# Attention output products as split f32, half a pair of heads later

## The chip, the cores and the metric

The kernel runs on one core of a Trainium2 chip. The metric is the device time in microseconds (us). Its engines are TensorE (PE in the profile, its weight loads PEld), VectorE (DVE), ScalarE (ACT), GpSimd (POOL) and SyncE (SP, which issues most transfers). Each works through its own queue in order, and they meet at semaphores.

## What is computed

Four layers follow one another over x of 4 x 1024 x 256 in f32: a gated scan, a layer of eight experts with two chosen per token, a causal attention with 16 heads of width 64, and a layer of 32 experts with four chosen. The change is in the attention:

```python
q = einsum('qdh,bcd->bhcq', Q, x) * sq
k = einsum('qdh,bcd->bhcq', K, x) * sq
v = einsum('vdh,bcd->bhcv', V, x) * sv
att = where(causal, einsum('bhcq,bhCq->bhcC', q, k) / d_query, -inf)
y = einsum('bhcC,bhCv->bhcv', softmax(att), v)
z = einsum('dvh,bhcv->bcd', W, y) * (sqrt(d_embed / d_value) / num_heads)
x = x + z
```

The last einsum is what is called the output products below: for every pair of heads (two heads of 64 values fill 128 rows) the normalised values y (128 x 1024, the tile `c_yT`) times the pair's part of W (128 x 256, the tile `c_wo`).

## The kernel before

The attention runs over 4 batches of 1024 tokens, each with 8 pairs of 2 heads. Its order is written out by hand for each engine, one function per head: `head_products` for TensorE, `head_steps` for VectorE, `head_exps` for ScalarE, `head_adds` for GpSimd, `head_operands` for SyncE. In the text an even head is the first of its pair (h = 0), an odd head the second (h = 1).

While head H has its probabilities made, its successors are already begun. On TensorE, one head is, in order: transposed score blocks 3, 4, 5 of H (`scores_t`, L2517 and L2518) between score chunks M4, M5, M6 of head H+1 (`scores`, L2494), projection steps 0, 1, 2 of head H+2 (`project`, L2481) around M7, the second half of the output products if the head is odd, M8, the denominators (L2546), four outputs y of H (`outputs`, L2537), blocks 6 to 8 with M9 to M11, four more outputs, a transpose of the row maxima (L2501), blocks 9 to 11, projection steps 3 to 5, the first four score chunks N0 to N3 of head H+2, blocks 0 to 2 of H+1, the last four outputs, and, if the head is even, the first half of the output products of the pair before (`z_of`, L2564).

A score chunk exists only so that VectorE can take its row maximum (`maximum`, L1873 for a plain chunk, L1880 for a masked one). Chunks, output products, denominators and some transposes take turns in a ring of three PSUM banks. The tables of `batch_order` and `turn_tables` deal out banks in the order in which the names stand, so M7 uses the bank of M4 again, whatever else comes before M4. TensorE may write a bank only after its last reader has added one to that bank's semaphore:

```python
pe.wait_ge(s_turn[use[0]], use[1])
pe.matmul(PS[:, TURN_BANK[use[0]], 0:max(w, 256)], ...).then_inc(s_cS, 1)
```

On VectorE the end of an even head is: maxima of N0 and N1, `normalise_y` of the pair before (L1893: c_yT times the inverses of the denominators, 128 x 1024), maxima of N2 and N3, two low parts of the next queries and keys (`split_lo`, L1851), and `add_z` of output products 0 and 1 (L1916: a bank added to two tiles of x). The next thing is the maximum of M4 for the following head. In the first batch a low part of projection weights (`low_qk`, L1856) stands between, and its high part (`high_qk`, L1190) closes the head on ScalarE.

On ScalarE the end of a head is the high parts of the next queries and keys (L1274) and the probabilities 0 to 2 of the next head (L1283); the next head begins with probability 3 and with taking y of the head before (L1265).

Output products are plain f32: one of them, 128 x 128 by 128 x 256, shows as two weight loads and two matmuls of 256 columns. There are 8 per pair, in 4 units of two. Products of split operands (high part rounded to f32r, low part the rest, three terms) are used for the projections and in the first expert stage (L2400 and L2403), where the high part is a ScalarE copy (L1140) and the low part a VectorE subtraction (L1742).

The last pair of a batch has its output products after the batch's heads, all four units in a row.

## Time and profile before

| | |
|---|---|
| time, median of 3 runs | 2092.15 us (2087.59 to 2097.59) |
| time of the profiled execution | 2105.81 us, its span 2104.1 us |
| busy share of the span: PE, PEld, DVE, ACT, POOL | 88%, 68%, 70%, 54%, 56% |
| attention, from about 665 to 1860 us | 1195 us |
| mean granted clock of TensorE | 0.937 |

The span is the time from the first to the last instruction of the profiled execution. Busy times of TensorE are of pipelined instructions, so the starts and ends of neighbours tell more than the duration of one.

### The profile page before, as it was taken

The page shows a single profiled execution, that of the slowest core. Times are in us where ns is not written, and L with a number is a line of the kernel's source. Part 1 is how long each engine was busy: PE and PEld are TensorE (multiplying, and loading weights), DVE is VectorE, ACT ScalarE, POOL GpSimd, SP SyncE. Part 2 cuts the span into 40 slices and gives each one's busy share as a digit, 9 for nine tenths or more (in the row PEclk, how much of TensorE's full clock was granted, in tenths as well). Part 3 has the DMA queues.
Part 4 walks back from the last instruction along what each step waited for, and adds up shares of the span by engine and source line. Part 5 has one row for each costly group of instructions (what it writes and reads, how often), then busy time and mean ns, then how long its engine had stood idle before and what let it go on. Part 6 is the DMA issues. An engine that isn't in the chain of part 4 may idle for free. (4 is left out here: it accounts for less than half of the span.)

```text
span 2104.1 us, 40780 instructions
## 1 busy us (share of the span) xinstructions
PE 1843.9 (88%) x12355; PEld 1438.9 (68%) x12356; DVE 1478.3 (70%) x3795; ACT 1141.9 (54%) x2322; POOL 1182.8 (56%) x1159
## 2 busy tenths in 40 slices
PE   5852999999779999999999999999999999973870
PEld 2542888888657677777777787777787777743650
DVE  6865777777567887756878756887757787653663
ACT  5322555555456566656665646656646656522760
POOL 4355232333306566636687836687836687825782
PEclk9865999999989999999999999999999999986995
DMA  9762533333331121202121102121211121122979
GB/s 338 244 206 88 129 51 54 51 53 53 61 110 52 56 59 52 61 26 60 46 82 52 50 28 60 52 58 44 53 30 54 52 59 52 30 95 84 200 127 262
DMA packets 215684, 177.34 MB, mean 84 GB/s; under 512 B 85442, under 2 KB 200727, under 8 KB 214880
## 3 DMA queue, kind: packets, MB, share of 16 engines
q1 hardware_dynamic: 177904, 138.78, 22.1%
q0 software_dynamic: 28656, 27.61, 8.5%
q10 hardware_dynamic: 8960, 8.92, 1.2%
q8 instruction: 84, 1.38, 0.3%
q14 instruction: 80, 0.66, 0.1%
HBM read 95.05 MB, written 80.72 MB: 84 GB/s over the span
## 5 line engine op out<-in xcount | busy, mean ns | idle before, releaser
L957 POOL TENSOR_TENSOR c_den_late<-c_den_late,c_p 128x512 f32<-128x512 f32 (+3 forms) x384 | 410.3, 1068 | 129.5 <-ACT c_p L1283 83.9
L1283 ACT ACTIVATE c_p<-PS 128x512 f32<-128x512 f32 (+3 forms) x768 | 343.2, 491 | 206.6 <-PE PS L2518 99.8
L2537 PE MATMUL PS<-c_p,c_vh 128*64 128x256 f32 (+3 forms) x3072 | 292.5, 333 | 0.5 <-ACT c_yT L1265 0.5
L2517 PE MATMUL PS<-c_q,c_k 128*128 128x512 f32 (+2 forms) x768 | 283.3, 373 | 2.8 <-ACT c_p L1283 1.7
L2494 PE MATMUL PS<-c_k,c_q 128*128 128x512 f32 (+2 forms) x768 | 268.6, 364 | 8.4 <-DVE c_max L1873 3.3
L2518 PE MATMUL PS<-c_q,c_k 128*128 128x512 f32 (+2 forms) x768 | 258.3, 348 | 0.0
L893 POOL DMA_INDIRECT acc<-b_y,b_tok x71 | 111.9, 1576 | 259.6 <-ACT b_y L1149 235.1
L2537 PEld LDWEIGHTS PS<-c_p,c_vh 128*64 128x64 f32 x3072 | 194.3, 137 | 87.6 <-issue 20.8
L1274 ACT ACTIVATE c_q<-PS 64x512 fp32r<-64x512 f32 x256 | 151.3, 591 | 158.2 <-PE PS L2481 147.0
L1873 DVE TENSOR_REDUCE c_max<-PS 128x1 f32<-128x512 f32 x256 | 175.3, 685 | 46.6 <-PE PS L2494 44.3
L957 POOL TENSOR_TENSOR c_den<-c_den,c_p 128x384 f32<-128x384 f32 (+2 forms) x192 | 141.4, 737 | 108.6 <-ACT c_p L1283 83.4
L1880 DVE CUSTOM_DVE_ANT_0 PS<-PS,c_maskq,c_max 128x128 f32<-128x128 f32 (+3 forms) x256 | 142.7, 558 | 82.5 <-PE PS L2494 47.9
L1880 DVE CUSTOM_DVE_ANT_0 PS<-PS,c_maskq 128x128 f32<-128x128 f32 (+3 forms) x256 | 122.5, 509 | 109.3 <-PE PS L2494 102.4
L2494 PEld LDWEIGHTS PS<-c_k,c_q 128*128 128x128 f32 x768 | 145.9, 190 | 46.9 <-DVE c_max L1873 8.8
L926 POOL DMA_INDIRECT routed<-r_rows,r_slot x128 | 128.6, 1004 | 61.7 <-DVEq L1992 34.4
L2517 PEld LDWEIGHTS PS<-c_q,c_k 128*128 128x128 f32 x768 | 144.7, 188 | 23.4 <-ACT c_p L1283 3.5
L2518 PEld LDWEIGHTS PS<-c_q,c_k 128*128 128x128 f32 x768 | 145.0, 189 | 8.9
L1742 DVE TENSOR_TENSOR b_w_lo<-b_w3T,b_w_hi 128x1024 fp32r<-128x1024 f32 x71 | 87.0, 1225 | 89.9 <-ACT b_w_hi L1140 89.9
L952 POOL TENSOR_TENSOR c_den_late<-c_p 128x512 f32<-128x512 f32 x64 | 81.4, 1272 | 100.1 <-PE PS L2546 82.8
L2381 PE MATMUL PS<-b_w12h,b_tT_hi 128*128 x284 | 124.0, 437 | 5.4 <-DVE b_tT_lo L1735 2.6
L2564 PE MATMUL PS<-c_wo,c_yT 128*128 128x256 f32 x512 | 124.6, 388 | 1.3 <-DVE c_yT L1893 1.3
L996 POOL DMA_INDIRECT acc<-d_y,d_tok x64 | 100.6, 1572 | 40.0 <-ACT d_y L1462 20.4
(313 smaller groups left out, 4345.7 us busy)
## 6 DMA issues: line engine op xcount, KB each, us to landing
c_vh<-c_v SPq DMA_DIRECT2D x64, 256.0 KB
c_rrow<-rden SPq DMA_DIRECT2D x63, 256.0 KB, 3.4
routed<-b_empty SPq DMA_DIRECT2D x32, 289.0 KB, 9.4
d_xe<-routed SPq DMA_DIRECT2D x32, 289.0 KB
b_xt<-routed SPq DMA_DIRECT2D x71, 130.0 KB, 2.1
b_w12T<-in_w12T_dram SPq DMA_DIRECT2D x16, 512.0 KB, 13.9
d_acc<-acc SPq DMA_DIRECT2D x16, 512.0 KB, 8.9
c_st_hi<-wqk_split SPq DMA_DIRECT2D x48, 128.0 KB
```

The source lines that it names most:

```text
L926: pool.indirect_dma_start(routed1, bass.IndirectOffsetOnAxis(ap=r_slot[n][:, j // K1, j % K1:j % K1 + 1], axis=0), r_rows[n][:, j // K1, : ...
L957: pool.tensor_tensor(den[:, off:], den[:, off:], p, ALU.add).then_inc(s_cPa, 1)
L1274: act.activation(dst, src, ACT.Copy).then_inc(s_cqs, 1)
L1283: act.activation(c_p[:, P_AT[h][m]:P_AT[h][m] + WIDTH[m]], PS[:, ST_BANK[m % STB], skip:skip + WIDTH[m]], ACT.Exp, scale=ATT_SCALE).then_i ...
L1873: dve.tensor_reduce(dst, src, AX_X, ALU.max).then_inc(s_turn[bank], 1)
L1880: dve.tensor_tensor_reduce(src, src, c_maskq[:, 512 - w:512], 1.0, dst if c else BIG, ALU.add, ALU.max, dst).then_inc(s_turn[bank], 1)
L2381: pe.matmul(PS[:, 2 * j + c, :], b_tT[0][:, j, k, :], b_w12h[k][:, cols], start=(k == 0), stop=False)
L2494: pe.matmul(PS[:, TURN_BANK[use[0]], 0:max(w, 256)], c_q1[h][:, t * P:(t + 1) * P], c_k1[h][:, c * 512:c * 512 + max(w, 256)], start=True, ...
L2517: pe.matmul(PS[:, bank, 0:n], c_k1[h][:, j * P:(j + 1) * P], c_q1[h][:, q], start=True, stop=False)
L2518: ins = pe.matmul(PS[:, bank, 0:n], c_k2[h][:, j * P:(j + 1) * P], c_q2[h][:, q], start=False, stop=not diagonal)
L2537: ins = pe.matmul(dst, c_vh[h][:, j, :], columns[:, :, a, :], start=(j == 0), stop=(t0 == 3))
L2564: ins = pe.matmul(PS[:, TURN_BANK[use[0]], a * D:(a + 1) * D], c_yT[q][:, t * P:(t + 1) * P], c_wo[q][:, :], start=True, stop=True)
```

## The change

The output products of all pairs but a batch's last are made of parts. ScalarE gets `split_y` at the end of each even head but a batch's first: it waits until the pair before is normalised, and copies c_yT and c_wo to their high parts `c_yTh` and `c_woh`. VectorE gets `low_y` in the place where `add_z` of units 0 and 1 stood: it waits for both copies and subtracts, to `c_yTl` and `c_wol`. TensorE runs `z_of_parts`, three products of 256 columns for each one of before, and later: units 0 and 1 stand in the odd head where units 2 and 3 stood, units 2 and 3 at the end of the odd head. `add_z` moves along, and the ring's tables with it. A batch's last pair stays as it was.

Beside this, tiles get other places in SBUF (`xn1` now shares memory with rows that are scattered, and `make_xn` waits for those scatters; `r_swb` shares memory with later tiles), and two semaphores of the first expert stage become one that ScalarE and VectorE raise in turn.

```diff
--- before.py
+++ after.py
@@ -242,7 +242,9 @@
         TURNS = len(TURN_BANK)
         Y_BANK = 6
         at[0] = arena_at
+        c_wol = [nc.alloc_sbuf_tensor_at(f"c_wo_lo_{n}", [P, D], F32R, offset=at[0] + n * 4 * D) for n in range(2)]
         c_wo = [place(f"c_wo_{n}", [P, D]) for n in range(2)]
+        c_woh = place("c_wo_hi", [P, D], F32R)
         c_xT = [place(f"c_xT{n}", [P, KD, S], F32R) for n in ("_hi", "_lo")]
         c_st = [[place(f"c_st{n}_{h}", [P, KD, P], F32R) for n in ("_hi", "_lo")] for h in range(2)]
         c_stf = [nc.alloc_sbuf_tensor_at(f"c_stf{h}", [P, KD, P], F32, offset=at[0] - 4 * KD * P * (3 - 2 * h)) for h in range(2)]
...
@@ -532,6 +536,10 @@
 
         ROUTE_AT = (0, 5)
 
+        def z_split(b, hp):
+
+            return b * (NPAIR - 1) + hp
+
         def batch_order(route, nxt):
 
 
@@ -540,9 +548,9 @@
                 follows, more, zs = nxt or hd < NH - 1, nxt or hd < NH - 2, hd >= 2
                 fetch = nxt and hd == NH - 2
                 order = ["M4", "M5", "M6"] * follows + ["X0", "X1", "D"] * fetch + ["M7"] * follows
-                order += ["Z2", "Z3"] * (zs and hd % 2 == 1) + ["M8"] * follows + ["D"] * (hd > 0 and not fetch)
+                order += ["Z0", "Z1"] * (zs and hd % 2 == 1) + ["M8"] * follows + ["D"] * (hd > 0 and not fetch)
                 order += ["M9", "M10", "M11"] * follows + ["X2", "X3"] * fetch + ["T"] * follows
-                order += ["N0", "N1", "N2", "N3"] * more + ["Z0", "Z1"] * (zs and hd % 2 == 0)
+                order += ["N0", "N1", "N2", "N3"] * more + ["Z2", "Z3"] * (zs and hd % 2 == 1)
                 if route:
                     for a in ROUTE_AT:
                         order += ["U0", "U1"] * (hd == a) + ["U2"] * (hd == a + 1) + ["U3"] * (hd == a + 3)
...
@@ -1202,6 +1210,10 @@
 
                     act.wait_ge(s_dxs, batch * 32 - 32)
                     act.sem_inc(s_pass, 1)
+                if g == 1 and not (isinstance(batch, int) and batch <= 1):
+
+                    act.wait_ge(s_scat[0], (batch - 1) * (16 * G * K1) + SCAT0)
+                    act.sem_inc(s_pass, 1)
                 for q in range(G):
                     t = batch * QT + (g * G + q)
                     act.activation(xn[g][:, q, :], tile_of(t, 0), ACT.Identity, bias=shifts[:, bass.ds(t, 1)],
@@ -1264,6 +1276,16 @@
                     dst = yT[h * DQ:(h + 1) * DQ, c * 512:(c + 1) * 512].rearrange("p (t a q) -> p t a q", a=2, q=DQ)[:, :, a, :]
                     act.activation(dst, PS[a * DQ:(a + 1) * DQ, Y_BANK, c * 256:(c + 1) * 256].rearrange("p (t q) -> p t q", q=DQ),
                                    ACT.Copy).then_inc(s_cyn, 1)
+
+            def split_y(b, hp):
+
+                pair, k, n = b * NPAIR + hp, z_split(b, hp), hp % 2
+                act.wait_ge(s_cz, pair * (QT // 2) + QT)
+                act.wait_ge(s_cym, pair + 1)
+                act.sem_inc(s_pass, 1)
+                act.activation(c_yTh[:, :], c_yT[n][:, :], ACT.Copy).then_inc(s_cyp, 1)
+                act.wait_ge(s_cwo, pair * 16 + 16)
+                act.activation(c_woh[:, :], c_wo[n][:, :], ACT.Copy).then_inc(s_cyp, 1)
 
             def split_hi(H, h, c, part):
 
@@ -1341,6 +1363,8 @@
                 if follows:
                     for m in (0, 1, 2):
                         probabilities(H + 1, 1 - h, m)
+                if h == 0 and hp:
+                    split_y(b, hp - 1)
                 if splits(b, hd + 3):
                     high_qk(H + 3, pair + (1 + h), 1 - h)
                 if nxt and NH - 4 <= hd < NH - 2:
...
@@ -1906,6 +1930,13 @@
                     cols = slice(c * 512, (c + 1) * 512)
                     dve.wait_ge(s_cD, H + (3 + c + 1))
                     dve.tensor_tensor(yT[DQ:P, cols], yT[DQ:P, cols], PS[DQ:P, 4 + c, :], ALU.mult).then_inc(s_cym, 1)
+
+            def low_y(b, hp):
+
+                k, n = z_split(b, hp), hp % 2
+                dve.wait_ge(s_cyp, 4 * k + 2)
+                dve.tensor_tensor(c_yTl[n][:, :], c_yT[n][:, :], c_yTh[:, :].bitcast(F32), ALU.subtract).then_inc(s_cyp, 1)
+                dve.tensor_tensor(c_wol[n][:, :], c_wo[n][:, :], c_woh[:, :].bitcast(F32), ALU.subtract).then_inc(s_cyp, 1)
 
             def add_z(b, pair, units, table):
 
@@ -2040,7 +2071,7 @@
                     invert(H - 1, 1 - h, table)
                 maxima(7)
                 if h == 1 and zs:
-                    add_z(b, pair - 1, (2, 3), table)
+                    add_z(b, pair - 1, (0, 1), table)
                 maxima(8)
                 if hd and not fetch:
                     invert(H - 1, 1 - h, table)
@@ -2068,7 +2099,9 @@
                 for k in range(2 * more):
                     split_lo(H + 2, h, 1, k)
                 if h == 0 and zs:
-                    add_z(b, pair - 1, (0, 1), table)
+                    low_y(b, hp - 1)
+                if h == 1 and zs:
+                    add_z(b, pair - 1, (2, 3), table)
                 if splits(b, hd + 3):
                     low_qk(H + 3, 1 - h)
                 routing(4)
...
@@ -2565,6 +2598,19 @@
                                     c_wo[q][:, :], start=True, stop=True)
                 ins.then_inc(s_cz, 1)
 
+            def z_of_parts(b, hp, n, use):
+
+                k, q = z_split(b, hp), hp % 2
+                pe.wait_ge(s_turn[use[0]], use[1])
+                pe.wait_ge(s_cyp, 4 * k + 4)
+                for a in range(2):
+                    rows = slice((2 * n + a) * P, (2 * n + a + 1) * P)
+                    z = PS[:, TURN_BANK[use[0]], a * D:(a + 1) * D]
+                    pe.matmul(z, c_yTh[:, rows], c_woh[:, :], start=True, stop=False)
+                    pe.matmul(z, c_yTh[:, rows], c_wol[q][:, :], start=False, stop=False)
+                    ins = pe.matmul(z, c_yTl[q][:, rows], c_woh[:, :], start=False, stop=True)
+                ins.then_inc(s_cz, 1)
+
             def transpose_rows3(g, n, table):
 
                 pe.wait_ge(s_dxn, g * G + G)
@@ -2615,7 +2661,7 @@
 
                 def z_units(*units):
                     for n in units * zs:
-                        z_of(pair - 1, 1 - hp % 2, n, table[f"Z{n}"])
+                        z_of_parts(b, hp - 1, n, table[f"Z{n}"])
 
                 def outputs_of(r):
                     for m in range(r * ROUND, (r + 1) * ROUND):
@@ -2642,7 +2688,7 @@
                     maxima(7)
                     projections(1)
                     if h == 1:
-                        z_units(2, 3)
+                        z_units(0, 1)
                     projections(2)
                     maxima(8)
                     if hd:
@@ -2683,10 +2729,8 @@
                         scores_t(H + 1, 1 - h, m)
                     mask_t(0, 1, 2)
                 outputs_of(2)
-                if h == 0 and zs:
-
-                    pe.wait_ge(s_cym, pair)
-                    z_units(0, 1)
+                if h == 1:
+                    z_units(2, 3)
                 if route:
                     for n, a in enumerate(ROUTE_AT):
                         g = b * 2 + (n - 2)
```

## Rows read from the trace of the kernel before

**Rows 1.** Windows of the attention: busy us of each engine (x instructions), granted clock.

```profile
core 0: us, PE busy (x) PEld busy (x) DVE busy (x) ACT busy (x) POOL busy (x), PEclk, DMA share, GB/s
...
665.00:930.00 265.00, 256.96 (x1872) 194.21 (x1872) 202.72 (x449) 160.71 (x353) 164.12 (x170) 1.00 0.19 53
...
1242.00:1555.00 313.00, 310.04 (x2259) 240.70 (x2258) 230.28 (x552) 191.40 (x411) 215.56 (x224) 1.00 0.18 49
```

**Rows 2.** TensorE's own waits over the four batches (two of the list).

```profile
engine line waited for: us in total, times, longest us
PE PS L2501 <- DVE c_max L1880: 8.0, 6, 1.8
...
PE PS L2494 <- DVE c_max L1873: 1.7, 3, 0.8
```

**Rows 3.** Timeline of TensorE, end of an even head: start us, us, line, count.

```profile
900.79 1.31 PE L2537 MATMUL PS<-c_p,c_vh 128*64 128x256 f32 x16
902.03 2.00 PE L2564 MATMUL PS<-c_wo,c_yT 128*128 128x256 f32 x8
...
904.14 0.48 PE L2494 MATMUL PS<-c_k,c_q 128*128 128x512 f32 x1
...
906.19 0.28 PE L2494 MATMUL PS<-c_k,c_q 128*128 128x256 f32 x1
906.31 0.63 PE L2481 MATMUL PS<-c_xT_hi,c_st_lo 128*128 128x512 f32 x2
906.77 1.89 PE L2564 MATMUL PS<-c_wo,c_yT 128*128 128x256 f32 x8
```

**Rows 4.** Timeline of VectorE, the same stretch.

```profile
899.77 1.42 DVE L1893 TENSOR_TENSOR c_yT<-c_yT,c_rrow 128x1024 f32<-128x1024 f32 x1
...
902.94 0.69 DVE L1851 TENSOR_TENSOR c_k<-PS,c_k 64x512 fp32r<-64x512 f32 x1
903.67 1.29 DVE L1916 SCALAR_TENSOR_TENSOR X<-PS,X 128x512 f32<-128x512 f32 x2
904.87 0.68 DVE L1873 TENSOR_REDUCE c_max<-PS 128x1 f32<-128x512 f32 x1
```

**Rows 5.** Timeline of ScalarE, the same stretch.

```profile
901.01 1.25 ACT L1283 ACTIVATE c_p<-PS 128x512 f32<-128x512 f32 x3
```

**Rows 6.** Timeline of TensorE, first expert stage: first row before, last of twelve.

```profile
500.99 0.38 PE L2370 MATMUL PS<-ident,b_xt 128*128 128x128 f32 x2
...
502.15 0.63 PE L2403 MATMUL PS<-b_w_hi,b_hT_lo 128*128 128x256 f32 x4
```

**Rows 7.** By line over the run, count, then min/median/max ns of one.

```profile
L2400 PEld LDWEIGHTS PS<-b_w_hi,b_hT_hi x284: 186/188/193, 212.6 to 566.8; 128*128 128x128 f32 x142
...
L1140 ACT ACTIVATE b_w_hi<-b_w3T x71: 1056/1060/1065, 208.2 to 563.6; 128x1024 fp32r x71
...
L1190 ACT ACTIVATE c_st_hi<-c_stf x16: 403/428/429, 587.5 to 864.1; 128x256 fp32r<-128x256 f32 x16
...
L1893 DVE TENSOR_TENSOR c_yT<-c_yT,c_rrow x31: 1224/1418/2705, 680.0 to 1830.0; 128x1024 f32<-128x1024 f32 x31
...
L2222 DVE TENSOR_TENSOR d_eh_lo<-d_eh,d_eh_hi x32: 405/417/425, 1939.5 to 2047.9; 128x256 fp32r<-128x256 f32 x32
```

**Rows 8.** Timeline of VectorE, end of an even head of the first batch.

```profile
683.92 1.29 DVE L1916 SCALAR_TENSOR_TENSOR X<-PS,X 128x512 f32<-128x512 f32 x2
685.13 0.72 DVE L1856 TENSOR_TENSOR c_st_lo<-c_stf,c_st_hi 128x256 fp32r<-128x256 f32 x1
685.77 0.68 DVE L1873 TENSOR_REDUCE c_max<-PS 128x1 f32<-128x512 f32 x1
```

**Rows 9.** Timeline of TensorE in that stretch.

```profile
686.50 0.39 PE L2494 MATMUL PS<-c_k,c_q 128*128 128x256 f32 x1
```

**Rows 10.** Timeline of GpSimd, the stretch of groups 3 to 5.

```profile
903.74 0.73 POOL L957 TENSOR_TENSOR c_den<-c_den,c_p 128x256 f32<-128x256 f32 x1 [0.17 <-issue]
```

More of the change, by code:

```diff
@@ L264, in network @@
         c_rrow = place("c_rrow", [P, S])
+        c_yTl = [nc.alloc_sbuf_tensor_at(f"c_yT_lo_{n}", [P, S], F32R, offset=at[0] + n * 4 * S) for n in range(2)]
         c_yT = [place(f"c_yT_{n}", [P, S]) for n in range(2)]
-        xn = [None, place("xn1", [P, G, D])]
-        c_spread = nc.alloc_sbuf_tensor_at("c_spread", [P, 4, NC2, DQ], F32, offset=at[0] - 4 * G * D)
+        c_spread = nc.alloc_sbuf_tensor_at("c_spread", [P, 4, NC2, DQ], F32, offset=at[0])
+        c_yTh = place("c_yT_hi", [P, S], F32R)
         after_heads = at[0]
-        R_BYTES = 27200
+        R_BYTES = 24576
         at[0] = top_at = (arena_end - 4 * 2 * KD * NH * DQ) // 32 * 32
@@ L276, in network @@
         assert after_heads <= r_at
-        r_swb = place("r_swb", [P, KD * E1 + KD * 2 * I1 + D], BF16)
         r_gwT = place("r_gwT", [P, KD, E1])
@@ L281, in network @@
         r_bias = place("r_bias", [P, 1, E1])
+        xn = [None, nc.alloc_sbuf_tensor_at("xn1", [P, G, D], F32, offset=at[0])]
         r_rows = [place(f"r_rows{n}", [P, G, W_ROW]) for n in range(2)]
@@ L290, in network @@
         r_idx = place("r_idx", [P, G * K1, 1])
+        r_swb = nc.alloc_sbuf_tensor_at("r_swb", [P, KD * E1 + KD * 2 * I1 + D], BF16, offset=at[0])
         r_oh = place("r_oh", [P, G, K1, E1])
@@ L421, in network @@
         s_cym = sem("c_y_normalised")
+        s_cyp = sem("c_y_and_weights_parts_ready")
         s_cz = sem("c_z_ready")
@@ L2393, in second_layer @@
                 pe.wait_ge(s_bhT, n + 1)
-                pe.wait_ge(s_w3l, n + 1)
+                pe.wait_ge(s_w3p, n * 2 + 2)
                 pe.wait_ge(s_bye, n + 1)
```

9 lines of the change are left out of this document (4 added, 5 removed).

## Prediction

> **What bounds the kernel now.** I read the windows first. Over the attention TensorE is busy 97 to 99% of each batch, VectorE 74 to 76%, ScalarE about 61%, at full granted clock [rows 1]. So whatever TensorE saves it saves for the whole, unless another engine then stops it. The view of its waits says that none does today: its largest wait on VectorE is 8.0 us in 1195, and waits of a score chunk for the plain maximum come to 1.7 us [rows 2]. A share of 75% says nothing of the moment, though, so I laid the timelines of the three engines over one another where the change works: the end of an even head, at 902 us, in a pair that looks like most others [rows 3 to 5].
>
> There the reader is to see two things. TensorE finishes its last outputs at 902.1, does output products until about 904, then M4 (904.14) to M7 (906.19) [rows 3]. VectorE has no gap from 899.77 to 905.55: normalise, two maxima, two low parts until 903.63, two additions until 904.96, and the maximum of M4 from 904.87 to 905.55 [rows 4]. M7 goes into M4's bank and may not start before that maximum is done. It started 0.64 us after it. That distance is all the slack there is, and the output products in front of M4 are part of what keeps it.
>
> **TensorE's own cost.** In the middle of the odd head the ends are clean: the matmul before ends at 906.31 + 0.63 = 906.94, the eight f32 matmuls (four output products) at 906.77 + 1.89 = 908.66: 1.72 us [rows 3]. The new form of four products is twelve matmuls of 256 columns, each with a weight load of its own. The first expert stage has exactly twelve in a row, the same shape, type and order of operands: the transposes before end at 501.37, the twelve at 502.15 + 0.63 = 502.78, so 1.41 us [rows 6]. It saves 0.31 us per half pair, 0.62 per pair. Changed are 7 pairs in each of 4 batches, 28: 17.4 us.
>
> Each weight load of those twelve lasts 188 ns in the profile [rows 7], but twelve take 1.41 us, 117 ns each, so loads lie under one another and under matmuls here. The Trainium skill (Perfetto Trace Analysis, Identifying the Most-Contended Engine) wants TensorE's headroom judged by the busy share of weight loads rather than of matmuls. By that rule, which speaks against this change, 24 loads a pair for 16 are a step back. The trace does not agree here: one by one, 24 loads would take 4.5 us a pair, and at the spacing of the expert stage they take 2.8.
>
> **ScalarE's cost.** A copy of 128 x 1024 to the high part took 1.06 us (L1140), one of 128 x 256 0.43 (L1190) [rows 7]. 1.49 us a pair is little for an engine busy 61%; what matters is when. It comes after the third probability, which ends at 901.01 + 1.25 = 902.26 [rows 5]; the normalised values are there since 901.19 [rows 4]. So both copies are ready at 903.75. Behind them stand probability 3 and the taking of y; their first reader on TensorE is the outputs after the denominators, more than 5 us on, so ScalarE's part costs TensorE nothing. If that cover were gone it could cost the 1.49.
>
> **VectorE's cost.** The low parts are 128 x 1024 and 128 x 256. For the first the bounds are L1893, a two-operand f32 pass of that size between SBUF tiles in this very stage: 1.22 shortest, 1.42 median, 2.71 longest; for the second L2222, 0.42 [rows 7]. I take 1.42, since GpSimd adds beside it now as it does beside normalise: it has an add at 903.74 [rows 10]. In this place VectorE had the two additions, 1.29 us; these move to the odd head.
>
> VectorE is free at 903.63, waits for ScalarE until 903.75, and ends the low parts at 903.75 + 1.42 + 0.42 = 905.59. Neighbours on VectorE overlap by some 0.06 (normalise to the next maximum), so say 905.5. The maximum of M4 is then done at 905.5 + 0.68 = 906.2.
>
> **The new wait.** TensorE comes to M4 earlier by the output products that no longer stand there, 1.72 us. Without a wait it would reach M7 at 906.19 - 1.72 = 904.47. It finds M4's bank in use until 906.2 and waits 1.7 us. Queued behind M7 are projection steps, the output products and everything after, so nothing hides it. M5 and M6 do not wait: their banks were N2's and N3's, whose maxima come before the low parts that end at 903.63. Put otherwise: M7 starts when it started before, since VectorE sets it. What was taken off TensorE in front of it is filled with idling, and the same work is done again at the end of the odd head.
>
> After M7 VectorE has M5, M6, M7, then additions of units 0 and 1. Z0 wants M5's bank, Z1 M6's, M8 M7's; counted with the present spacings each is free 0.1 us or more before TensorE comes, and VectorE is at M8 again where it was before. At the end of the odd head there is no normalise, so VectorE is 1.4 us earlier relative to TensorE, and the output products before M4 give it more room still: no wait there.
>
> The sum for a pair: -3.44 (two halves in f32) + 2.82 (two halves of parts) + 1.7 (wait) = +1.08 us. Times 28: +30.2.
>
> In the first batch M4's maximum also stands behind a low part of weights, and there M7 starts at 686.50, 0.05 us after that maximum's end [rows 8, 9]. With no slack to give, six pairs pay some 0.5 us more: +3. In the routed batches some M7 are already that close and one per batch has more slack; I let these cancel. The odd rest of the last batch (no M4 left to wait for, but the output products then wait for the low parts) has about the same price as the others.
>
> **Other edits, costed at nothing.** The two semaphores made one order the same two steps. The wait of make_xn is for scatters of heads 6 to 9, and it stands in head 13; if they were late, GpSimd's queue would stop ScalarE. SyncE's fetch of the next c_wo waits for units now half a head later, and the staging of a head's values is queued behind it; it has the 5 us up to that head's first outputs and more. The additions moved cover no new wait: each stands two chunks ahead of the next use of its bank. The total is +33 us. The profiled execution would go from 2105.8 to about 2139; the median of the runs lies 13.7 us below it, so I add the difference to the median: 2092.15 + 33 = 2125.
>
> **Rivals.**
> (a) *Low parts are hidden: faster.* If VectorE finished M4 by 904.5, TensorE would keep the full 17.4 us: 2075. Place: the end of the even head. It decides at a wait of 0.62 us a pair, below which the change gains. For it speaks that VectorE idles a quarter of the time, and that nothing but order ties it. Against: its queue has no gap there [rows 4], and low parts must be 1.1 us shorter than their nearest rows. Chance 0.12.
> (b) *Partly hidden: no change.* The wait is 0.3 to 1.0 us, because the fastest rows hold (1.22 for the low part) and VectorE comes out of normalise sooner. From -9 to +11 us: 2083 to 2103. Chance 0.10.
> (c) *The wait as worked out, +22 to +48.* With 1.22 for every low part the wait is 1.5: +0.88 x 28 = +25. With 1.9, between median and longest, it is 2.2: +1.6 x 28 = +45. Chance 0.70.
> (d) *GpSimd is pushed back: slower yet.* A low part longer than 1.42 delays GpSimd's adds as well, and with them denominators; at the longest row, 2.71, the pair would pay 3.0 for 1.7: +2.4 x 28 = +67, near 2160. The routed batches, where GpSimd is busy 69%, would show it. The Trainium skill (SBUF — State Buffer, Who interferes with whom) says that VectorE and GpSimd share one pair of ports under an exclusive lock; normalise between 1.22 and 2.71 on one shape [rows 7] agrees with it. Chance 0.05.
> (e) *Weight loads go one by one.* 12 x 0.188 = 2.26 for 1.41 a half pair: +1.7 a pair on top of (c), +80, 2172. Against it stand the twelve of rows 6. Chance 0.03.
>
> **How the numbers follow.** The likeliest is (c) at 2125; its own range is 2112 to 2141. The whole range keeps 8 in 10 by taking the upper part of (b): 2096 to 2143. A measurement of this kernel can tell about 0.5%, 10.5 us, from no change. Faster is (a), 0.12. Within it is (b), 0.10. Slower are (c), (d) and (e), 0.78.
>
> **What would show it.** In the profile after: the twelve matmuls of a half pair in 1.4 us; low parts of 1.4 and 0.4 us right before the maximum of M4; a wait of L2494 for c_max (L1873) near 1.7 us about 27 times, some 45 us in the list of TensorE's waits where there were 1.7; no such wait in even heads; TensorE's busy share in the attention down to about 93%. I am wrong if M7 starts as soon as the projection before it ends; then the low parts were shorter or earlier than their rows say. I am wrong in size if the wait is there and TensorE also waits at Z0, at the denominators, or for ScalarE's probabilities.

## The result, and the profile after

The changed kernel takes 2124.27 us (median of 4 runs, 2120.67 to 2126.69), the kernel before 2089.87 us on the same chip (median of 4, 2086.80 to 2097.59). The ratio is 1.015, with a 95% interval of 1.0133 to 1.0168: slower, by some 31 us by the ratio and 34 by the two medians. The forecast was 2125 us.

The execution that was profiled took 2124.02 us, its span is 2122.3. Line numbers have moved: score chunks are L2527 (L2494 before), projections L2514, the transpose of the maxima L2534, the three products of the parts L2609 to L2611, the low parts of keys and queries L1875, the plain maximum L1897, the masked one L1904, the low parts of c_yT and c_wo L1938 and L1939.

The windows of the attention first, the same stretches as in [rows 1]:

```profile
core 0: us, PE busy (x) PEld busy (x) DVE busy (x) ACT busy (x) POOL busy (x), PEclk, DMA share, GB/s
665.00:930.00 265.00, 244.21 (x1844) 186.59 (x1845) 204.00 (x439) 161.86 (x352) 163.25 (x163) 0.99 0.18 49
...
1242.00:1555.00 313.00, 301.49 (x2255) 232.89 (x2254) 236.62 (x555) 194.18 (x413) 217.74 (x219) 0.99 0.18 49
```

TensorE's busy share fell from 97.0 to 92.2% in the first window and from 99.1 to 96.3% in the second, at a granted clock of 0.99 for 1.00. So it is hardly slowed, it is kept waiting. For what, its list of waits says (line that waited, releaser: us in total, times, longest), over the attention as in [rows 2]:

```profile
PE PS L2527 <- DVE c_k L1875: 25.8, 24, 1.5
PE PS L2527 <- DVE c_max L1897: 10.2, 15, 1.3
PE PS L2514 <- DVE c_st_lo L1880: 6.8, 6, 1.6
PE PS L2534 <- DVE c_max L1904: 5.4, 3, 1.8
PE PS L2527 <- DVE r_tmp L1989: 4.1, 3, 1.4
...
PE PS L2609 <- DVE c_wo_lo L1939: 1.7, 1, 1.7
```

All are waits for VectorE. The one for the plain maximum, which the forecast had at some 45 us, is the second of the list with 10.2. The first is one that the forecast does not have: score chunks that wait for the low part of the keys (`c_k`). Both are seen in the timeline of TensorE at the end of the same even head as in [rows 3]:

```profile
901.28 1.31 PE L2570 MATMUL PS<-c_p,c_vh 128*64 128x256 f32 x16
...
902.87 0.23 PE L2558 MATMUL PS<-c_maskk,identb 128*128 128x128 bf16 x1
904.18 0.50 PE L2527 MATMUL PS<-c_k,c_q 128*128 128x512 f32 x1 [1.08 <-DVE c_k L1875]
...
905.81 0.62 PE L2514 MATMUL PS<-c_xT_hi,c_st_hi 128*128 128x512 f32 x2
907.04 0.38 PE L2527 MATMUL PS<-c_k,c_q 128*128 128x256 f32 x1 [0.61 <-DVE c_max L1897]
907.26 0.62 PE L2514 MATMUL PS<-c_xT_hi,c_st_lo 128*128 128x512 f32 x2
907.73 0.30 PE L2609 MATMUL PS<-c_wo_hi,c_yT_hi 128*128 128x256 f32 x1
...
909.04 0.28 PE L2611 MATMUL PS<-c_wo_hi,c_yT_lo 128*128 128x256 f32 x1
```

and in the timeline of VectorE for it, to be held against [rows 4]:

```profile
900.26 1.41 DVE L1917 TENSOR_TENSOR c_yT<-c_yT,c_rrow 128x1024 f32<-128x1024 f32 x1
...
903.43 0.69 DVE L1875 TENSOR_TENSOR c_k<-PS,c_k 64x512 fp32r<-64x512 f32 x1
904.15 1.23 DVE L1938 TENSOR_TENSOR c_yT_lo<-c_yT,c_yT_hi 128x1024 fp32r<-128x1024 f32 x1
905.30 0.97 DVE L1939 TENSOR_TENSOR c_wo_lo<-c_wo,c_wo_hi 128x256 fp32r<-128x256 f32 x1
906.30 0.69 DVE L1897 TENSOR_REDUCE c_max<-PS 128x1 f32<-128x512 f32 x1
```

M4 (904.18) starts 0.06 us after the low part of the keys ends (903.43 + 0.69 = 904.12), and M7 (907.04) starts 0.05 us after M4's maximum ends (906.99). Before, eight f32 matmuls stood between the last outputs and M4, and by the time they were done the keys were split, so that this wait did not show.

Counted from the start of the last outputs (900.79 before, 901.28 after), VectorE ends the low part of the keys 2.84 us later in both kernels. TensorE without a wait would start M4 at 902.87 + 0.04 = 902.91, for in the kernel before M4 starts 0.04 us after that same mask matmul (904.10 and 904.14). So it waits 1.27 us there; the list says 1.08, since it counts from the modelled end of the matmul before. At M7 it would have been ready 0.47 us after the projection step of 905.81 (as 907.26 to 907.73 shows), at 906.28, and waits 0.76. Together 2.0 us in this pair, and M7 starts 5.76 us after the outputs for 5.40 before.

To compare whole kernels I take the attention from the start of its first score chunk to the start of its last block of transposed scores. By line (count, min/median/max ns of one, first and last start), the kernel before:

```profile
L2494 PE MATMUL PS<-c_k,c_q x768: 273/388/502, 604.0 to 1826.0; 128*128 128x512 f32 x128, 128*128 128x256 f32 x64
...
L2518 PE MATMUL PS<-c_q,c_k x768: 276/364/403, 631.7 to 1845.0; 128*128 128x512 f32 x192
```

and the changed one:

```profile
L2527 PE MATMUL PS<-c_k,c_q x768: 274/387/796, 594.0 to 1848.0; 128*128 128x512 f32 x128, 128*128 128x256 f32 x64
...
L2551 PE MATMUL PS<-c_q,c_k x768: 276/364/402, 621.7 to 1867.0; 128*128 128x512 f32 x192
```

1241.1 us before, 1273.0 after: +31.9, as much as the ratio says. The two profiled executions differ by 18 us only, mostly because the attention of the one before begins 10 us later; the other 4 us lie behind the attention. (That execution, 2105.81 us, lies outside the four runs that give the median before.) The start seems to go with the chip and not with the kernel: in the four kernels of the first group below it is 606.4, 606.5, 608.0 and 609.0, the last made from the kernel before and the others from the changed one; in all later ones it is 589 to 595. Why the stages ahead differ by chip was not tried.

### The profile page after: what moved, and what is told of

It reads as the page before. It is cut to its first block and busy times, and to the rows that moved or that the text cites. A ratio compares the mean times of both kernels' runs of the same rounds, so it can differ in the third digit from the quotient of the medians.

```text
span 2122.3 us, 41430 instructions
## 1 busy us (share of the span) xinstructions
PE 1831.7 (86%) x12579; PEld 1429.6 (67%) x12580; DVE 1522.3 (72%) x3851; ACT 1175.3 (55%) x2378; POOL 1207.2 (57%) x1159
## 3 DMA queue, kind: packets, MB, share of 16 engines
q8 instruction: 86, 1.41, 0.3%
## 5 line engine op out<-in xcount | busy, mean ns | idle before, releaser
L2527 PE MATMUL PS<-c_k,c_q 128*128 128x512 f32 (+2 forms) x768 | 269.8, 366 | 42.8 <-DVE c_k L1875 25.8
L965 POOL TENSOR_TENSOR c_den<-c_den,c_p 128x384 f32<-128x384 f32 (+2 forms) x192 | 158.3, 825 | 111.6 <-ACT c_p L1305 85.0
L2527 PEld LDWEIGHTS PS<-c_k,c_q 128*128 128x128 f32 x768 | 145.6, 190 | 88.0 <-DVE c_k L1875 29.8
L1904 DVE CUSTOM_DVE_ANT_0 PS<-PS,c_maskq,c_max 128x128 f32<-128x128 f32 (+3 forms) x256 | 143.0, 559 | 85.4 <-PE PS L2527 50.8
L1904 DVE CUSTOM_DVE_ANT_0 PS<-PS,c_maskq 128x128 f32<-128x128 f32 (+3 forms) x256 | 122.5, 509 | 111.3 <-PE PS L2527 111.0
L1897 DVE TENSOR_REDUCE c_max<-PS 128x1 f32<-128x512 f32 x256 | 175.5, 685 | 34.3 <-PE PS L2527 32.4
L1148 ACT ACTIVATE b_w_hi<-b_w3T 128x1024 fp32r x71 | 75.3, 1060 | 80.9 <-PE PS L2436 80.7
```

The costliest lines, as they stand in the source:

```text
L965: pool.tensor_tensor(den[:, off:], den[:, off:], p, ALU.add).then_inc(s_cPa, 1)
L1897: dve.tensor_reduce(dst, src, AX_X, ALU.max).then_inc(s_turn[bank], 1)
L1904: dve.tensor_tensor_reduce(src, src, c_maskq[:, 512 - w:512], 1.0, dst if c else BIG, ALU.add, ALU.max, dst).then_inc(s_turn[bank], 1)
L2527: pe.matmul(PS[:, TURN_BANK[use[0]], 0:max(w, 256)], c_q1[h][:, t * P:(t + 1) * P], c_k1[h][:, c * 512:c * 512 + max(w, 256)], start=True, ...
```

## The experiments

Kernels ran in three groups, and the kernel before took 2111.31, 2094.46 and 2092.30 us in them. A ratio is always to the kernel before of the same group. The whole in a table, in the order in which they are told:

| kernel | median, us | ratio (95% interval) | attention, us | against before |
|---|---|---|---|---|
| the change | 2124.27 | 1.0150 (1.0133 to 1.0168) | 1273.0 | +31.9 |
| the change, other chip | 2121.09 | 1.0124 (1.0103 to 1.0145) | 1275.0 | +33.9 |
| f32 products, moved | 2123.08 | 1.0050 (1.0033 to 1.0067) | 1254.5 | +13.4 |
| parts at the old places | 2098.20 | 0.9929 (0.9908 to 0.9951) | 1230.0 | -11.1 |
| the change, low parts of 8 columns | 2106.67 | 0.9977 (0.9965 to 0.9989) | 1240.2 | -0.9 |
| normalised later | 2216.48 | 1.0483 (1.0453 to 1.0512) | 1356.3 | +115.2 |
| f32 products, moved, normalised later | 2089.35 | 0.9971 (0.9959 to 0.9983) | 1238.0 | -3.1 |
| low parts in the odd head's gap | 2111.83 | 1.0087 (1.0067 to 1.0108) | 1252.8 | +11.7 |
| the same in three pieces | 2104.94 | 1.0059 (1.0041 to 1.0077) | 1253.6 | +12.5 |
| gap, low parts of 8 columns | 2087.66 | 0.9969 (0.9955 to 0.9982) | 1233.6 | -7.5 |

The last two columns come from one profiled execution of each kernel, and from the one trace of the kernel before. The change itself gave 1273.0 and 1275.0. Against the differences of the medians they are off by 7 us or less (10 in the slowest), most of all in the change on the other chip (+33.9 for +26.6) and in the odd head's gap, whose profiled execution was the fastest of its four (+11.7 for +17.4). So differences of a few us in these columns say little.

**The move alone.** The output products are f32 as before, and stand where the change has them. Nothing is split.

```diff
-                if h == 0 and hp:
-                    split_y(b, hp - 1)
...
-                if h == 0 and zs:
-                    low_y(b, hp - 1)
...
+                    if zs and 0 in units:
+                        pe.wait_ge(s_cym, pair)
...
-                        z_of_parts(b, hp - 1, n, table[f"Z{n}"])
+                        z_of(pair - 1, 1 - hp % 2, n, table[f"Z{n}"])
```

> The output products stay f32 as before, and nothing is split; only their place changes to that of the changed kernel (units 0 and 1 in the middle of the odd head, 2 and 3 at its end). Theory A, the working of the prediction: a bare end of the even head costs nothing by itself, the wait comes from the low parts in front of the maximum of M4. Without them that maximum ends about 904.4 and M7 wants its bank at 904.5: no wait, 2090 us (2086 to 2094). Theory B, from the trace of the changed kernel: M4 also waits for the low part of the keys (1.08 us idle, 24 such waits), which the two f32 output products used to cover. Then the move alone costs some 1.2 us in each of 28 pairs: about 2122 us (2116 to 2126), with the wait of scores for c_k in the list.

It is slower by 0.5%, 12 us by the medians. Theory B has the kind of wait right and its size not: 2123.08 us looks like its 2122, but the kernel before took 2111.31 in this group, so B's 28 x 1.2 = 34 us came out as 12. TensorE's list of waits, of this kernel:

```profile
PE PS L2523 <- DVE c_k L1873: 25.6, 24, 1.4
```

The wait for the keys is here in full, 24 times, and there is none for the plain maximum: with no low parts in its way, VectorE ends M4's maximum in time. So this wait belongs to the move, the other to the low parts. It is 25.6 us by the list, but the attention grew by 13.4 only. Most of the difference shows in the list of the kernel before. The 8.0 us of the transpose of the maxima and the 1.7 of M7 in [rows 2] are 5.4 and none here, and these waits are gone:

```profile
PE PS L2494 <- DVE c_xT_lo L1843: 2.6, 6, 0.6
...
PE PS L2564 <- DVE c_yT L1893: 1.3, 3, 0.4
...
PE PS L2494 <- DVE X L1916: 1.0, 3, 0.3
```

2.6 + 1.7 + 2.6 + 1.3 + 1.0 = 9.2 us of idling that a TensorE held up earlier in the pair no longer meets. 25.6 - 9.2 = 16.4, for 13.4 measured. The rest, 3 us or some more since the list counts each wait short (1.08 for 1.27 above), was not followed.

**The parts alone.** Made from the kernel before, at its old places: each f32 product becomes three f32r products of 256 columns. They read other tiles of f32r that are there anyway (`c_xT`, `c_wv`), so the values of the output products are left out, and nothing has to be split for them.

```diff
-                    ins = pe.matmul(PS[:, TURN_BANK[use[0]], a * D:(a + 1) * D], c_yT[q][:, t * P:(t + 1) * P],
-                                    c_wo[q][:, :], start=True, stop=True)
+                    z = PS[:, TURN_BANK[use[0]], a * D:(a + 1) * D]
+                    if parts:
+                        for k in range(3):
+                            ins = pe.matmul(z, c_xT[0][:, 0, t * P:(t + 1) * P], c_wv[0][:, 0, 0:D],
+                                            start=(k == 0), stop=(k == 2))
...
```

> The kernel before, where each output product of all pairs but a batch's last is three f32r products of 256 columns at the old places. Nothing is split: the operands are tiles that are already rounded (c_xT_hi and c_wv_hi), so the values are left out and only TensorE's time is right. Weight loads hidden (the prediction's term): 0.31 us less in the middle of the odd head and up to 0.31 at the end of the even one, less where M7 is already close to its bank: 14 to 17 us less than before, about 2075 us. Weight loads one by one: 2 us more per pair, 2140 us or more.

0.7% faster, 11 to 15 us, where the sum had 17.4 at most. The form of the product is a gain, and TensorE does keep most of what it saves as long as nothing else moves.

**Low parts of 8 columns.** The change as it is, but the two subtractions work on 8 columns in place of 1024 and 256, and the products that read low parts read high parts.

```diff
-                dve.tensor_tensor(c_yTl[n][:, :], c_yT[n][:, :], c_yTh[:, :].bitcast(F32), ALU.subtract).then_inc(s_cyp, 1)
-                dve.tensor_tensor(c_wol[n][:, :], c_wo[n][:, :], c_woh[:, :].bitcast(F32), ALU.subtract).then_inc(s_cyp, 1)
+                dve.tensor_tensor(c_yTl[n][:, 0:8], c_yT[n][:, 0:8], c_yTh[:, 0:8].bitcast(F32), ALU.subtract).then_inc(s_cyp, 1)
+                dve.tensor_tensor(c_wol[n][:, 0:8], c_wo[n][:, 0:8], c_woh[:, 0:8].bitcast(F32), ALU.subtract).then_inc(s_cyp, 1)
...
```

> The changed kernel, with both subtractions of low_y done on 8 columns only, and the three products of a part all made of the high parts; so the low parts are left out and the output products are only high times high, three times over. TensorE and ScalarE have the same work as in the changed kernel, VectorE 2.1 us less per pair. Theory A: the wait goes altogether, 28 x 1.6 = 45 us less than the changed kernel, about 2079 us. Theory B: only the second wait (M7 for its bank, about 0.6 us) goes, the 1.2 us at M4 stay: about 2107 us (2103 to 2111).

Its list of waits begins, within the attention, with

```profile
PE PS L2527 <- DVE c_k L1875: 25.9, 24, 1.5
```

and has none for the plain maximum. The attention is 32.8 us shorter than with whole low parts. So the second wait is VectorE's time for the low parts, and that time is the largest term of the change. The kind of wait is that of Theory B, the size that of neither theory: less than the change by 17 us (B) or 45 (A), measured 32.8. (2106.67 us is near B's 2107 only because the kernel before was some 20 us slower in this group.) By the lists 22.8 of the 32.8 are waits that are gone: 10.2 of M7 and, with the low parts ahead of them, 6.8 for `c_st_lo`, 4.1 for `r_tmp` and 1.7 for `c_wo_lo`; the rest is not in the list. From the move alone (+13.4) to here (-0.9) lies what the parts save again, 14.3 us. The three terms are +13.4 for the move, -14.3 for the form of the products, +32.8 for the low parts.

**Normalised later.** If the keys are what M4 waits for, they should be split ahead of the normalisation. Here `normalise_y` stands behind `split_lo`, with `low_y` right behind it, and all else is the change.

```diff
                 maxima_ahead(0, 1)
-                if h == 0 and zs:
-                    normalise_y(pair - 1, c_yT[1 - hp % 2])
                 routing(3)
...
                     split_lo(H + 2, h, 1, k)
                 if h == 0 and zs:
+                    normalise_y(pair - 1, c_yT[1 - hp % 2])
                     low_y(b, hp - 1)
```

> The changed kernel, with the normalisation of y moved behind the two low parts of queries and keys. The keys' low part is then ready before M4 wants it, but ScalarE's copies start 2.5 to 3 us later, and VectorE waits for them in front of the maximum of M4. Theory B (and A): VectorE's chain up to that maximum sets M7; it grows from 906.99 - 902.59 = 4.4 us after the last outputs to about 6.0: 1.5 x 28 = 42 us more than the changed kernel, about 2166 us (2150 to 2175), with no wait for c_k and one of 2.3 us or more at M7. Theory C, that only the wait for the keys' low part costs time and the bank of M4 nothing: 33 us less than the changed kernel, 2091 us.

The direction was as expected, the size not. The list of TensorE's waits:

```profile
PE PS L2526 <- DVE c_max L1897: 53.5, 18, 3.6
PE PS L2513 <- DVE c_st_lo L1880: 24.2, 6, 4.8
PE PS L2526 <- DVE r_tmp L1989: 12.9, 3, 4.3
```

The wait for the keys has gone, and the others are long, since VectorE now stands before the low parts until ScalarE has made its copies of what was just normalised: 43.4 us in 28 times by its own list. These waits come to 91 us against 49 in the change, which explains half of the 83 us by which this attention is longer. The other part is mostly the clock. TensorE after one such wait, its timeline:

```profile
1041.85 0.39 PE L2526 MATMUL PS<-c_k,c_q 128*128 128x256 f32 x1 [3.18 <-DVE c_max L1897]
...
1042.78 0.28 PE L2610 MATMUL PS<-c_wo_hi,c_yT_lo 128*128 128x256 f32 x1
...
1043.58 0.41 PE L2610 MATMUL PS<-c_wo_hi,c_yT_lo 128*128 128x256 f32 x1
...
1044.43 1.05 PE L2513 MATMUL PS<-c_xT_lo,c_st_hi 128*128 128x512 f32 x2
```

and the windows around it, with the granted clock in the third column from the end, and of a long stretch:

```profile
1041.00:1043.00 2.00, 1.16 (x7) 0.98 (x8) 1.72 (x5) 0.04 (x1) 0.96 (x1) 1.00 0.00 0
1043.00:1047.00 4.00, 4.00 (x31) 2.86 (x31) 2.49 (x6) 1.18 (x2) 0.00 (x0) 0.57 0.00 0
...
700.00:1900.00 1200.00, 1110.38 (x8095) 863.28 (x8092) 856.44 (x1992) 699.75 (x1495) 759.92 (x767) 0.96 0.17 47
```

After 3.18 us of idling the clock falls to its lower level of 1.2 GHz for most of 4 us, and matmuls that took 0.28 us take 0.41, projection pairs 1.05 for 0.63. Over 1200 us the mean clock is 0.96, so some 48 us of full speed are lost (with the rounding of that figure, 42 to 54), where the change, with waits of at most 1.8 us in the attention, shows 1.00 (700 to 1860 us).

**The move, normalised later, nothing split.** The remedy for the first wait without the second cost: f32 products at the new places, `normalise_y` behind `split_lo`.

```diff
                 maxima_ahead(0, 1)
-                if h == 0 and zs:
-                    normalise_y(pair - 1, c_yT[1 - hp % 2])
                 routing(3)
...
                 for k in range(2 * more):
                     split_lo(H + 2, h, 1, k)
                 if h == 0 and zs:
-                    low_y(b, hp - 1)
+                    normalise_y(pair - 1, c_yT[1 - hp % 2])
```

> As e3_move_alone (f32 output products at the new places, nothing split), and the normalisation of y stands behind the two low parts of queries and keys at the end of the even head. The move alone cost 12 us more than the kernel before, with 24 waits of M4 for the keys' low part. If that wait is only a matter of VectorE's order, it goes, and since the maximum of M4 still ends where it did, about when M7 wants the bank, nothing takes its place: 0 to 5 us less than the kernel before (ratio 0.997 to 1.000). If the 12 us come from elsewhere (another order of banks, output products beside other work), the ratio stays near 1.005.

The list of waits:

```profile
PE PS L2530 <- DVE c_max L1902: 5.4, 3, 1.8
...
PE PS L2510 <- DVE c_st_lo L1878: 4.3, 6, 1.2
```

No chunk waits for keys, and the attention is 16.5 us shorter than with the move alone. That settles the first wait: it was the order of VectorE's queue, with normalise's 1.41 us ahead of the keys. This kernel, which computes everything, is faster than both: by 0.3% than the one before. It also holds all the other edits (places in SBUF, joined semaphores, the wait of `make_xn`), so these cost nothing that shows; no kernel has them alone.

**Low parts in the odd head's gap.** A proposal: ScalarE's copies and the subtractions half a head later, ahead of the maxima of N0 and N1 of the odd head; all four units of products at that head's end; normalised later as above.

```diff
                 routing(2)
+                if h == 1 and zs:
+                    low_y(b, hp - 1)
                 maxima_ahead(0, 1)
...
-                        z_units(0, 1)
...
                 if h == 1:
-                    z_units(2, 3)
+                    z_units(0, 1, 2, 3)
```

> All of the change, put into gaps of the queues: normalisation behind the low parts of queries and keys at the end of the even head; ScalarE's two copies in the odd head behind probabilities 4 and 5, where it idled 2.7 us; VectorE's two subtractions in the odd head in front of the maxima of N0 and N1, where it idled 1 to 2 us; all four units of output products at the end of the odd head. If both waits (M4 for the keys' low part, M7 for its bank) were only of order, the 0.62 us per pair that TensorE saves come through: 13 to 17 us less than the kernel before in this chip's time, ratio 0.992 to 0.994. In the first batch a low part of weights still stands in front of M4, which may cost up to 3 us. If the low parts cost their 2 us of VectorE wherever they stand, the ratio is 1.00 or more.

It fails: 1.0087. VectorE there:

```profile
1034.96 1.88 DVE L1938 TENSOR_TENSOR c_yT_lo<-c_yT,c_yT_hi 128x1024 fp32r<-128x1024 f32 x1 [0.15 <-DVE r_slot L2021]
1036.77 0.41 DVE L1939 TENSOR_TENSOR c_wo_lo<-c_wo,c_wo_hi 128x256 fp32r<-128x256 f32 x1
```

and TensorE:

```profile
1037.62 0.51 PE L2525 MATMUL PS<-c_k,c_q 128*128 128x512 f32 x1 [1.18 <-DVE c_max L1904]
```

N3 needs N0's bank, whose maximum now stands behind 2.2 us of low parts. It is the same wait as at M7, at another place: 15.9 us in 19 times. The list has a second one, for the transpose of the maxima: 12.4 us in 8 times, the longest 2.55, where the kernel above has 5.4. It comes back below.

**The same in three pieces.** c_wo's low part goes behind the inverses, the first half of c_yT's ahead of N0, the second ahead of the additions, and the normalisation behind `low_qk`. The edit is shown against the kernel just above.

```diff
+                if h == 1 and zs:
+                    low_y(b, hp - 1, 0)
...
                 routing(2)
                 if h == 1 and zs:
-                    low_y(b, hp - 1)
+                    low_y(b, hp - 1, 1)
...
                 if h == 1 and zs:
+                    low_y(b, hp - 1, 2)
                     add_z(b, pair - 1, range(4), table)
```

> Parts and low parts are computed in the odd head, and all four units of output products stand at the odd head's end. The two subtractions are now three pieces (the one of wo behind the inverses; the first half of the one of c_yT ahead of N0's maximum; its second half behind the low parts of the keys, ahead of add_z), and the normalisation stands behind low_qk. Theory E (what costs is one block of 2.3 us ahead of N0's maximum, for which N3's bank is late): the 19 waits of N3 of 1.7 us shrink to under 0.5 us each, and the ratio to the kernel before is 0.990 to 0.994. Theory F (each low part costs its full time on VectorE wherever it stands, since a pass of two operands also shuts GpSimd out, and VectorE's queue has no slack left in either head): the waits move to other matmuls (transpose of the maxima, M7, first projection of the next head) and the ratio is 1.000 or more.

The waits of N3 shrink to at most 0.3 us, as Theory E has it, and the time does not follow. The list of TensorE's waits has others instead:

```profile
PE PS L2538 <- DVE c_max L1904: 24.1, 15, 4.0
PE PS L2531 <- DVE c_max L1897: 10.3, 6, 1.8
```

The transpose of the maxima (L2538) and M7 now wait, and the attention is as long as in one piece (1253.6 and 1252.8 us; by the ratios it is 0.3% shorter). Theory E is out: the ratio is 1.0059 and not below 0.994. That is no proof of Theory F, though. The six waits of M7 are all in the first batch, where no low part of the output products stands ahead of M4's maximum, but `low_qk` and, behind it now, the normalisation:

```profile
750.19 1.24 DVE L1880 TENSOR_TENSOR c_st_lo<-c_stf,c_st_hi 128x256 fp32r<-128x256 f32 x1
751.35 1.78 DVE L1917 TENSOR_TENSOR c_yT<-c_yT,c_rrow 128x1024 f32<-128x1024 f32 x1
```

These waits of M7 take the place of the 4.3 us for `c_st_lo` in the orders above. And 12 of the 24.1 us of the transpose are three waits of 3.95, one in each routed batch (batches 2 to 4, in which VectorE also routes tokens for the next layer), of which the next kernel shows the cause.

**The gap with low parts of 8 columns.** The order of the proposal in one piece, with the subtractions narrowed as above (the outputs lack the low parts).

```diff
-                dve.tensor_tensor(c_yTl[n][:, :], c_yT[n][:, :], c_yTh[:, :].bitcast(F32), ALU.subtract).then_inc(s_cyp, 1)
+                dve.tensor_tensor(c_yTl[n][:, 0:8], c_yT[n][:, 0:8], c_yTh[:, 0:8].bitcast(F32), ALU.subtract).then_inc(s_cyp, 1)
...
```

> The order of e5_parts_in_gaps, but the low parts have 8 columns in place of 1024 and 256, and the second and third products take the high parts (the outputs lack the low parts). It says what the order would be worth if the low parts were free. Theory E and F alike: no wait for a maximum's bank above 0.3 us, attention some 14 us shorter than with the f32 products moved and normalised late (0.9971), so 0.989 to 0.992. If instead the order itself (all four units at one place) is what costs, it stays at 1.000 or more, and the low parts are not to blame in e5.

0.9969: better than with whole low parts by 1.2%, 19.2 us of attention, but short of the 0.989 to 0.992 that both theories had. N3's 15.9 us of waits are gone. TensorE's list of waits still shows

```profile
PE PS L2532 <- DVE c_max L1904: 14.3, 9, 2.6
```

for the transpose, 9 us more than in the kernel with the late normalisation and nothing split. Once in each of three batches it is 2.56 to 2.58 us long, and TensorE's clock falls behind it, as the window after one of them (1105.20) shows:

```profile
1105.00:1110.00 5.00, 4.80 (x21) 4.28 (x22) 1.92 (x10) 1.59 (x5) 2.89 (x4) 0.66 0.01 1
```

0.34 of 5 us is 1.7 us more, three times. 9 and 5 us come to 14, and with them the row above for the late normalisation (-3.1) and the form (-14.3) gives -3, for -7.5 measured. So the order has a price of its own, at one place per routed batch, and the low parts are no part of it: with whole ones the same three waits are 2.55 us each. What VectorE does ahead of the late maximum is two passes of the routing over 4 columns, at 1098.29 and 1100.39:

```profile
1098.29 1.55 DVE L1996 COPY r_rows<-tokens 128x4 uint32<-128x4 uint32 x1
...
1100.39 1.95 DVE L2001 TENSOR_SCALAR r_ws<-r_ws 128x4 f32<-128x4 f32 x1
```

In the kernel before, the change and the late normalisation with nothing split they never take more than 0.38 and 0.17 us. Here GpSimd is at its additions meanwhile (1098.52 and 1101.01, 1.29 us each), and the passes end 0.03 and 0.04 us after them, at 1099.84 and 1102.34. So 3 us of VectorE standing still make this transpose late. In the three pieces c_wo's low part (1.98 us there) and the same copy (2.02) stand in a row, and the wait is 3.95. Whether the place of the units or that of ScalarE's copies brought these passes beside the additions stays open. And the narrow subtractions are not free here, by line:

```profile
L1938 DVE TENSOR_TENSOR c_yT_lo<-c_yT,c_yT_hi x28: 152/822/1093, 686.6 to 1824.0; 128x8 fp32r<-128x8 f32 x28
```

Eight columns take 152 ns at best and 822 in the median, and the pass right behind it, over 8 columns of c_wo, 154. One of them, in the timeline of VectorE:

```profile
1211.98 1.08 DVE L1938 TENSOR_TENSOR c_yT_lo<-c_yT,c_yT_hi 128x8 fp32r<-128x8 f32 x1
```

and of GpSimd:

```profile
1211.75 1.29 POOL L965 TENSOR_TENSOR c_den_late<-c_den_late,c_p 128x512 f32<-128x512 f32 x1 [0.17 <-POOL c_den_late L965]
```

VectorE's pass of 8 columns ends at 1213.06, GpSimd's addition at 1213.04. It did not run, it stood until GpSimd was done. The narrow kernel thus is no measure of free low parts in this place.

**The change again**, on the chip of the second group:

> The changed kernel itself once more, so that it has a time beside the kernel before on this chip too. Both theories: 1.5% more than the kernel before, 1.013 to 1.017 of it.

The ratio is 1.0124 here for 1.015, just under what was expected, the attention +33.9 for +31.9, and TensorE's list of waits is the same to within 0.3 us per line.

## Why the prediction was right, and where it was not

The time, the sign and the sum held. One wait was ascribed to the wrong instruction, in part, and the time was met partly by luck, since two terms were off in opposite directions.

**TensorE's own cost.** Twelve matmuls of parts: the one before ends at 907.26 + 0.62 = 907.88, the last of the twelve at 909.32, 1.44 us for 1.41. Saved per pair 0.56 for 0.62. In whole kernels the form of the products is worth 11.1 us of attention at the old places and 14.3 at the new, for 17.4. With 24 weight loads a pair for 16, the loads were busy 76.0% of the attention in the kernel with the parts alone and 75.6% in the one before, and the time fell. Rival (e), weight loads one by one, is excluded by the twelve.

**ScalarE's cost.** The two copies took 1.07 and 0.43 us, and began at 902.62, 0.13 us earlier than forecast when counted from the outputs. As forecast they cost TensorE nothing that shows where they stand: its waits for ScalarE's probabilities (1.0 us) and for y (0.5) are those of before. The order with the normalisation right before the low parts shows what is lost when that cover goes: VectorE waits for them 43.4 us.

**VectorE's cost.** The first low part took 1.23 for 1.42, the second 0.97 for 0.42. By line over the changed kernel:

```profile
L1938 DVE TENSOR_TENSOR c_yT_lo<-c_yT,c_yT_hi x28: 1224/1226/1883, 673.9 to 1856.7; 128x1024 fp32r<-128x1024 f32 x28
...
L1939 DVE TENSOR_TENSOR c_wo_lo<-c_wo,c_wo_hi x28: 676/956/969, 675.0 to 1857.9; 128x256 fp32r<-128x256 f32 x28
```

Together 2.18 us for 1.84: a term mis-sized by 0.34, and in its distribution. I had put GpSimd's presence on the long pass and none on the short. GpSimd's addition, 0.73 us in [rows 10], shows why:

```profile
904.23 1.75 POOL L965 TENSOR_TENSOR c_den<-c_den,c_p 128x256 f32<-128x256 f32 x1 [0.17 <-ACT c_p L1305]
```

It begins 0.08 us after VectorE's long low part, which runs undisturbed to 905.38, and ends at 905.98, 0.60 us after it; the short low part begins at 905.30 and ends at 906.27. The two took turns. The Trainium skill (SBUF — State Buffer, Who interferes with whom) says that a VectorE instruction with two inputs in SBUF contends with a GpSimd instruction that reads SBUF, and that the one that comes first holds the shared ports for its whole instruction while the other stands still; the traces agree, most plainly the 1.08 us of 8 columns.

**The new wait.** "Without a wait it would reach M7 at 904.47" is the step that failed. I followed the bank of M7 and did not ask what else M4 waits for: `scores` waits for the split keys too (`s_cks`, in chunks 0 and 4), and the f32 products ahead of M4 had covered that. M4 cannot start before 904.18, so it takes the larger share, 1.27 us, and M7 0.76. The sum, 2.0 us in the pair for 1.7, differs little, because M7 must in any case come after a maximum that stands at a fixed place in VectorE's queue. "M7 starts when it started before, since VectorE sets it" is right as to who sets it, and 0.36 us off as to when, of which 0.28 is the later end of the low parts (4.99 us after the outputs for 4.71).

That the sum agrees is no proof of the account, and two experiments show it was incomplete. By the account the move alone should not wait; it waits 25.6 us. And with 8 columns the wait should vanish; half of it stayed.

**The sum.** +1.08 us times 28 and 3 for the first batch, 33 us; measured 31.9 and 33.9 in the attention, 1.5 and 1.2% in the ratios. The terms behind it are others: the move costs 13.4 where I had no term for it, with part of its wait given back where TensorE used to wait before; the low parts cost 32.8 where the forecast comes to 33 + 17.4 = 50; the form saves 14.3 for 17.4. That the first two errors and the small third cancel to 1 us is luck in the number, though not without reason: both waits end where VectorE's queue stands. The first batch, put at 3 us, has waits of its own: projections wait 6.8 us for `c_st_lo`, which stands behind the low parts there as the forecast said of M4's maximum, and M7 itself is not in the list there.

**What would show it.** No output product waits at the end of an odd head, as forecast; the one that waits (1.7 us, once) is in the middle of the last odd head, where the forecast has output products wait for the low parts. TensorE's busy share of about 93% is met in the first batch (92.2%) and not in the third (96.3%). Some 45 us were to be added to TensorE's waits on VectorE; the five lines that are new or longer sum to 25.8 + 10.2 + 6.8 + 4.1 + 1.7 = 48.6. In the form given, 27 waits for the plain maximum near 1.7 us, it is wrong: 15, of 0.7 us on average.

**The other edits** were costed at nothing, and the kernel with all of them and a ratio of 0.9971 bears that out. **Rival (a)**, low parts hidden, is what the orders with late splits tried to reach. The low parts took 61, 75 and 93 us of VectorE's time in the change, in the odd head's gap and in three pieces. Against the same order with 8 columns they cost 32.8 us of attention in the first and 19.2 in the second; the third has no such kernel beside it.

## What to carry to other kernels

When work is taken out in front of an instruction, list every semaphore that this instruction waits for, and place each releaser in time; the one that ends last may be one that the removed work has hidden. An engine that is busy three quarters of the time can still have no room where a bank must be freed, and moving or cutting a block there can move the wait in place of removing it. Before VectorE passes that read two SBUF operands are added, look at what GpSimd does at that moment: here the passes paid for both engines.

## What the hardware showed that was not expected

A VectorE pass with two SBUF operands can take the rest of a GpSimd addition on top of its own time: 8 columns took 152 ns at best, 822 in the median and 1093 at most in the odd head's gap, while the same pass in the even head's place took 169 in the median and 819 at most. It is not only passes with two operands: the copy of 4 columns above took 0.37 us in the median and 1.57 at most, the pass with one operand over 4 columns 0.17 and 1.95.

A stall of TensorE of 3.18 us was followed by half clock for most of 4 us, and one of 2.56 us by a mean of 0.66 over the next 5; in the attention of the kernel before and of the changed one, from the first score chunk to the last transposed block, where the longest waits were 1.8 us, it stayed at 0.99 to 1.00. Behind that last block the kernel before has one wait of 3.81 us (1850.65, for GpSimd), and there too the mean clock fell, to 0.67 from 1850 to 1855. Where such a wait is added, its price is more than its length: matmuls of 256 columns started 0.21 us apart for 0.12.
